# A two-layer recurrence with experts: column pairs, half-tile deal, fixed slots and paced loads

## The chip, the core and the metric

The kernel runs on one core of a Trainium2 chip. The time is the device time of one execution in microseconds (us). The median of the kernel before is 1176.22 us over three runs, from 1175.07 to 1176.29 us.

## What is computed

The input `x` has 16 sequences of 256 steps with 256 features. Four layers follow each other, each adding to `x`:

```
h_t = tanh(h @ Wh + x_t @ Wx + b)                       # plain recurrence, 256 steps
i,f,o,g = split(x_t @ Wx + b + h @ Wh)                  # LSTM, 256 steps
c = sigmoid(f)*c + sigmoid(i)*tanh(g);  h = sigmoid(o)*tanh(c)
out = gelu(x @ sw1 + sb1) @ sw2 + sb2                   # shared expert
    + sum over the 2 chosen of 4 experts: w * (gelu(x @ ew1[e] + eb1[e]) @ ew2[e] + eb2[e])
w = gelu(layernorm(cond) @ W1 + bias1) @ W2 + bias2     # low-rank parts of an adapter
x + up(gelu(down(x)))                                   # adapter, matrices per sequence
```

All products are made of float16 numbers: a float32 value is held as a high part (HI) and a remainder (LO), and one product takes three matmuls, HI by HI, LO weights by HI data, and HI weights by LO data.

## The kernel before, in words

**Two recurrences side by side.** Time is cut into 16 blocks of 16 steps (`U`). After a head that transposes `x` and runs the plain recurrence (RNN) on block 0, the main loop `block_steps` runs the LSTM on block `it`, the RNN on block `it + 1`, and the shared expert on block `it - 1`. Each of the 256 loop steps has the same skeleton.

- TensorE (`lstm_step`, `rnn_step`): 48 narrow matmuls of 16 columns for the eight LSTM gate tiles, then 12 for the RNN. It then adds wide work that depends on nothing recent: `fig_x` and `o_x` (the input parts of the LSTM gates, 64 and 128 columns), and tiles of the shared expert (`shared_hidden`, `shared_down`, six matmuls of 256 columns each) as the table `FILL` deals them. At the end of a block `rnn_x(it + 2)` makes the input part of a whole RNN block: 14 matmuls of 256 columns.
- ScalarE (L537, L541, L548): tanh of six gate tiles (`tfig`), tanh of the output gate (`to`), then `rnn_step` (L531, L532: `rf` in float32 and `RH` in float16), then tanh of the cell (`tc`), then whatever else the step has: seeds of PSUM banks (L555), two GELUs of a hidden tile (L581 into `gel`, L584 into `GH`), a weight piece to its high part (L497).
- VectorE (`lstm_step`, L846 to L858): `fc`, `ig` and the cell from `tfig`; after `tc` the high part of the hidden state (L851, semaphore `v_hh`), for which TensorE's next step waits, then its low part and the sum into `X`. Behind these stand remainders of hidden tiles (L824), remainders of weight pieces (L731), the splitting of `X` for the expert (L795, L798, at step 0), `add_y` (L818, at step 15).
- GpSimd: the low part of the RNN's hidden state (L406) and four small sums a step.

**Experts' weights.** Four experts have two matrices of 1 MB each. In blocks 1 to 8 one matrix per block is turned into HI and LO in eight pieces, at the steps 2, 4, 5, 6, 7, 9, 11 and 12 (`EXPERT_WINDOWS`). SyncE loads a whole matrix of 1 MB into `stage0` when the previous one is used up. In the same blocks, which I call matrix blocks, a part of the adapter's `W2` (1 MB, into `stage1`) is multiplied at steps 12 and 13 (`low_rank`, eight float32 matmuls), `add_bias` (VectorE, L946) and `low_hi` (ScalarE, L629) follow at step 14, and `low_lo` (VectorE, L952) at step 15. Blocks 9 to 13 have neither; I call them plain blocks.

**After the loop.** The gate chooses two experts per sequence, and these experts and the adapter follow, from about 754 us to the end. The change does not touch their code.

What orders the work is the program order on each engine and the semaphores between engines; there is no scheduler. Each engine takes its instructions in order.

Of the kernel before, what the change touches and what calls it, by code (L numbers as in the profile page):

```python
# [19 lines left out]
F32 = mybir.dt.float32  # L20
# [6 lines left out]
P = 128  # L27
B, T, D = 16, 256, 256
C = D // P
U = 16  # L30
NB = T // U
G = 8
# [25 lines left out]
def build_program(nc, a, out, scratch):  # L58
    ctx = ExitStack()
    with ctx:  # L60
# [35 lines left out]
        rf = sb("rf", [P, 2, C, B], F32)  # L96
        x1s = sb("x1s", [P, 2, C, B], F32)
# [58 lines left out]
        def late(*shape):  # L156
# [43 lines left out]
        names = """ld_stage0 ld_stage1 ld_small ld_first ld_cond ld_bias ld_rnn  # L200
# [4 lines left out]
            a_xr p_xr pe_rx pe_r a_rh  p_rlo p_x1 p_x1h p_x1l  # L205
# [38 lines left out]
        EXPERT_WINDOWS = (2, 4, 5, 6, 7, 9, 11, 12)  # L244
# [46 lines left out]
        def _(sp):  # L291
            with nc.allow_non_contiguous_dma(reason="small tables, once"):
# [35 lines left out]
                for j in range(2 * E):  # L328
                    def load_expert():

                        sp.wait_ge(s["v_wlo"], SHARED_SPLIT + j * N_MATRIX if j else LSTM_SPLIT + N_MATRIX)
                        src = a[("L2_cond_ew1", "L2_cond_ew2")[j % 2]][j // 2]
                        sp.dma_start(stage[0][:, :].rearrange("p (c n) -> p c n", c=(C, M)[j % 2]), wide(src)
                                     ).then_inc(s["ld_stage0"], 16)

                    if j == 0:
                        load_expert()
                        sp.wait_ge(s["v_wlo"], SHARED_SPLIT)
                    else:
                        sp.wait_ge(s["pe_w2"], j)  # L340
                        sp.wait_ge(s["v_low"], j)
                    for t in range(4):
                        at = j * 1024 + t * LOW_N
                        sp.dma_start(low_bias[32 * t:32 * t + 32, :],
                                     a["L3_cond_bias2"][at:at + LOW_N].partition_broadcast(2 * B)
                                     ).then_inc(s["ld_bias2"], 16)
                    sp.dma_start(w2_in, wide(a["L3_cond_W2"])[:, :, j * 1024:(j + 1) * 1024]
                                 ).then_inc(s["ld_stage1"], 16)
                    if j > 0:
                        load_expert()  # L350
# [133 lines left out]
        def _(act):  # L484
# [40 lines left out]
            def rnn_step(blk, r):  # L525
                n = blk * U + r
                z = RB[:, :].rearrange("p (m t b) -> p m t b", m=C, t=U)[:, :, r, :]
                act.wait_ge(s["pe_r"], n + 1)
# [30 lines left out]
            def seeds(it, u, last):  # L559

                if u % H == H - 1 and not (last and u >= U - 2 * H):
                    seed(it * U + u + 1, FIG[u // H % 2], slice(0, 6), H, "a_fig_seed")
                if u % G == G - 1 and not last:
                    seed(it * U + u + 1, OB[u // G], slice(6, 8), G, "a_o_seed")

            def x_hi(blk, c):

                act.wait_ge(s["pe_rx"], blk)
# [9 lines left out]
            def shared_gelu(tile, m):  # L578
                act.wait_ge(s["pe_h"], tile + 1)
                act.wait_ge(s["v_gl"], tile - 1)  # L580
                nc.scalar.activation(gel[:, m % 2, :], HB[m % 2][:, 0:256], ACT.Gelu_apprx_tanh,  # L581
                                     scale=1 / S_W1, bias=sb1[:, m:m + 1])
                act.wait_ge(s["pe_d"], tile - 3)
# [15 lines left out]
            def block_steps(it, first, last, matrix=False):  # L599
                for u in range(U):  # L600
                    lstm_gates(it, u)
                    if not last:
                        rnn_step(it + 1, u)
                    lstm_cell(it, u)
                    seeds(it, u, last)
                    if not first:
                        for kind, m in FILL[u]:
                            if kind == "h":
                                shared_gelu(it * M + m, m)
# [10 lines left out]
                    if matrix and u in EXPERT_WINDOWS:  # L620
                        i = EXPERT_WINDOWS.index(u)
                        if i == 0:
                            act.wait_ge(s["ld_stage0"], it * 16 + 32)
# [1001 lines left out]
```

## Time and profile before

| | us |
|---|---|
| median of three runs | 1176.22 |
| profiled execution | 1176.01 |
| its span, first to last instruction | 1174.2 |
| TensorE (PE) matmuls busy | 1131.0, 96% of the span |
| VectorE (DVE) busy | 764.5, 65% |
| ScalarE (ACT) busy | 605.2, 52% |
| GpSimd (POOL) busy | 366.3, 31% |
| mean granted TensorE clock | 0.967 of full |

A busy TensorE is not TensorE at its peak, since consecutive matmuls overlap in the records. The time of a stretch is therefore read from the distance between starts of instructions, not from the busy time. One `tfig` instruction of ScalarE stands for one step of the loop, so that the first and last start of a count of them gives the time of so many steps.

### The profile page before, as it was taken

What the parts mean: (1) busy time and instruction counts of PE and PEld (TensorE: products, weight loads), DVE (VectorE), ACT (ScalarE), POOL (GpSimd) and SP (SyncE); (2) the same over time, 40 slices, a digit from 0 to 9 for tenths busy, and PEclk for the clock granted to TensorE, in tenths of its full rate; (3) what the DMA queues carried; (4) which work ended last, traced back from release to release, by engine and by line L of the source; (5) the groups of instructions that cost most, each with busy time, mean ns of one, the idle gap of its engine ahead of it and who ended that gap; (6) DMA issues with size and microseconds to landing.
All of it is one profiled execution on the core that took longest, in us unless ns stands there. A gap on an engine that the chain in (4) does not pass through costs nothing. (4 is left out here: it accounts for less than half of the span.)

```text
span 1174.2 us, 58158 instructions
## 1 busy us (share of the span) xinstructions
PE 1131.0 (96%) x23706; PEld 1010.7 (86%) x23706; DVE 764.5 (65%) x2954; ACT 605.2 (52%) x2147; POOL 366.3 (31%) x1372
## 2 busy tenths in 40 slices
PE   5899999999999999999999999899999999999998
PEld 4788889889889888999999998778888888888877
DVE  6565666666666656556565557687666666667697
ACT  4455566566566555565555554533333333334476
POOL 3654344344434334444444441065000000000041
PEclk7759999999989989999999999899999999999999
DMA  8211202202202011110000000000000000000022
GB/s 245 75 44 40 80 4 81 79 5 80 68 16 80 25 59 26 14 15 14 4 4 5 4 5 4 3 2 1 2 2 2 2 2 2 2 3 2 3 76 87
DMA packets 44432, 37.14 MB, mean 32 GB/s; under 512 B 24280, under 2 KB 39946, under 8 KB 44172
## 3 DMA queue, kind: packets, MB, share of 16 engines
q1 hardware_dynamic: 43564, 33.12, 9.3%
q8 instruction: 194, 3.18, 1.1%
q14 instruction: 66, 0.54, 0.2%
q10 hardware_dynamic: 608, 0.30, 0.1%
HBM read 28.42 MB, written 4.98 MB: 28 GB/s over the span
## 5 line engine op out<-in xcount | busy, mean ns | idle before, releaser
L1285 PE MATMUL bank<-LH,seq 128*128 128x16 f16 x8192 | 282.8, 170 | 12.2 <-DVE LH L851 10.0
L1285 PEld LDWEIGHTS bank<-LH,seq 128*128 128x128 f16 x8192 | 248.1, 96 | 53.9 <-DVE LH L851 46.5
L575 ACT ACTIVATE gel<-bank,seq 128x256 f32<-128x256 f32 x256 | 121.2, 473 | 215.1 <-PE bank L1190 212.2
L1188 PE MATMUL bank<-XHL,WE 128*128 128x256 f16 x768 | 211.1, 275 | 5.2 <-issue 3.0
L1188 PE MATMUL bank<-GH,WE 128*128 128x256 f16 x768 | 210.3, 274 | 1.6 <-DVE GH L824 1.2
L1190 PE MATMUL bank<-XHL,WE 128*128 128x256 f16 x768 | 211.2, 275 | 0.0
L1189 PE MATMUL bank<-XHL,WE 128*128 128x256 f16 x768 | 211.1, 275 | 0.0
L1189 PE MATMUL bank<-GH,WE 128*128 128x256 f16 x768 | 210.3, 274 | 0.0
L1190 PE MATMUL bank<-GH,WE 128*128 128x256 f16 x768 | 210.1, 274 | 0.0
L1291 PE MATMUL bank<-LH,seq 128*128 128x16 f16 x4096 | 177.2, 169 | 1.7 <-issue 1.7
L406 POOL TENSOR_TENSOR RH<-rf,RH 128x32 f16<-128x32 f32 x256 | 64.5, 252 | 354.1 <-ACT RH L532 354.1
L537 ACT ACTIVATE tfig<-bank 128x96 f32<-128x96 f32 x256 | 65.5, 256 | 208.9 <-PE bank L1291 206.6
L1189 PE MATMUL bank<-seq 128*128 128x64 f16 (+2 forms) x1024 | 156.0, 211 | 1.1 <-issue 1.1
L1190 PE MATMUL bank<-seq 128*128 128x64 f16 (+2 forms) x1024 | 157.0, 211 | 0.0
L1188 PE MATMUL bank<-seq 128*128 128x64 f16 (+2 forms) x1024 | 154.5, 210 | 0.0
L831 DVE CAST GH<-gel 128x256 f16<-128x256 f32 x256 | 78.3, 306 | 102.0 <-ACT gel L575 101.3
L1291 PEld LDWEIGHTS bank<-LH,seq 128*128 128x128 f16 x4096 | 139.4, 96 | 1.4 <-issue 1.4
L476 POOL TENSOR_TENSOR seq<-X,seq 128x512 f16<-128x512 f32 x16 | 21.5, 1344 | 332.1 <-ACT seq L650 332.1
L846 DVE SCALAR_TENSOR_TENSOR fc<-tfig,c 128x32 f32<-128x32 f32 x256 | 48.8, 191 | 114.2 <-ACT tfig L537 108.9
L833 DVE TENSOR_TENSOR GH<-gel,GH 128x256 f16<-128x256 f32 x256 | 113.0, 441 | 8.7
L851 DVE SCALAR_TENSOR_TENSOR LH<-to,tc 128x32 f16<-128x32 f32 x256 | 51.7, 202 | 77.4 <-ACT tc L548 77.4
L1190 PEld LDWEIGHTS bank<-seq 128*128 128x128 f16 x1024 | 97.6, 100 | 3.3 <-issue 1.2
(198 smaller groups left out, 2469.0 us busy)
## 6 DMA issues: line engine op xcount, KB each, us to landing
stage<-in_L_cond_ew SPq DMA_DIRECT2D x8, 1024.0 KB, 8.5
stage<-in_L_cond_W SPq DMA_DIRECT2D x8, 1024.0 KB, 5.3
XHL<-in_x SPq DMA_DIRECT2D x8, 512.0 KB, 9.2
out<-WE SPq DMA_DIRECT2D x16, 256.0 KB, 2.1
stage<-in_L_cond_sw SPq DMA_DIRECT2D x2, 1024.0 KB, 5.4
scratch<-rows SPq DMA_DIRECT2D x96, 8.0 KB, 2.3
stage<-in_L_cond_Wx SPq DMA_DIRECT2D x1, 1024.0 KB, 9.6
stage<-in_L_cond_Wh SPq DMA_DIRECT2D x1, 1024.0 KB, 11.8
```

Source lines behind the costliest of these rows:

```text
L406: nc.gpsimd.tensor_tensor(RH[:, slot, LO], rf[:, slot], RH[:, slot, HI], ALU.subtract).then_inc(s["p_rlo"], 1)
L537: nc.scalar.activation(tfig[:], FIG[u // H % 2][:, 0:6 * H * B].rearrange("p (m t b) -> p m t b", m=6, t=H)[:, :, u % H, :], ACT.Tanh, sca ...
L575: nc.scalar.activation(gel[:, m % 2, :], banks[m % len(banks)][:, 0:256], ACT.Gelu_apprx_tanh, scale=scale, bias=bias).then_inc(s["a_g"], 1)
L831: V.tensor_copy(GH[:, m % 4, HI], gel[:, m % 2]).then_inc(s["v_gh"], 1)
L833: V.tensor_tensor(GH[:, m % 4, LO], gel[:, m % 2], GH[:, m % 4, HI], ALU.subtract).then_inc(s["v_gl"], 1)
L846: V.scalar_tensor_tensor(fc[:], tf, 1.0, c2[:], ALU.add, ALU.mult)
L851: V.scalar_tensor_tensor(hh, to[:], 1.0, tc[:], ALU.add, ALU.mult).then_inc(s["v_hh"], 1)
L1188: MM(out_, w(HI), x(HI), start=start, stop=False, skip_group_check=True)
L1189: MM(out_, w(LO), x(HI), start=False, stop=False, skip_group_check=True)
L1190: return MM(out_, w(HI), x(LO), start=False, stop=stop, skip_group_check=True)
L1285: MM(z, LW[:, h, 1, c, tile * P:(tile + 1) * P], LH[:, old, HI, c], start=False, stop=False, skip_group_check=True)
L1291: last = MM(z, LW[:, HI, 1, c, tile * P:(tile + 1) * P], LH[:, old, LO, c], start=False, stop=(c == C - 1), skip_group_check=True)
```

## The change

There are six edits.

1. **Column pairs.** For the RNN blocks from 1 on (`PAIR_FROM`), the matmuls HI weights by HI data and HI weights by LO data become one matmul with 32 columns: the data `RH[:, old, :, c]` are both halves, and the two results go to two halves of the PSUM bank. A step has 8 RNN matmuls in place of 12. VectorE adds the two results (`rnn_sum`, a reduction from PSUM into the new SBUF tile `rz`), and ScalarE's `rf` and `RH` read `rz` and wait for `v_rz`.
2. **`rnn_x` in halves.** Since a bank now holds half a block, `rnn_x` runs twice a block, ahead of the RNN's matmuls of steps 0 and 8, with 14 matmuls of 128 columns each.
3. **Half-tile deal.** `FILL` comes from `HALVES`: a half tile is three matmuls of 256 columns, and each step has 0 to 3 of them, ahead of `fig_x`. `o_x` of the second half block moves from step 0 to steps 3 and 5.
4. **Fixed ScalarE slots.** Between `to` and `tc` stands now either the second GELU of the tile that was finished one step earlier (`shared_hi`) or a weight piece; `rf` and `RH` come after `tc`; then the first GELU (`shared_full`).
5. **Expert pieces over thirteen blocks.** Five pieces per block, at steps 1, 5, 7, 9 and 11, from block 1 to 13.
6. **Paced loads.** A piece of 128 KB is loaded into its part of `stage0` when the piece eight before it is used up; `W2` comes in four loads of 256 KB in a row, at the end of a block.

```diff
-        EXPERT_WINDOWS = (2, 4, 5, 6, 7, 9, 11, 12)
+        EXPERT_WINDOWS = (1, 5, 7, 9, 11)
...
+                def load_piece(i):
+                    j, k = divmod(i, N_MATRIX)
+                    sp.wait_ge(s["v_wlo"], SHARED_SPLIT + i + 1 - N_MATRIX if j else LSTM_SPLIT + k + 1)
...
+                    sp.dma_start(stage[0][:, at], src).then_inc(s[f"ld_e{k}"], 16)
...
+                ahead = N_MATRIX
+                for it in range(1, NB - 1):
+                    for k in range(5):
+                        if ahead < total:
+                            load_piece(ahead)
+                            ahead += 1
+                        if it < 2 * E and k == 5 - 1:
+                            for q in range(4):
+                                load_low_part(it, q)
...
+                    z = rz[:]
+                    act.wait_ge(s["v_rz"], n + 1 - PAIR_FROM * U)
...
                     lstm_gates(it, u)
+                    if not first and u > 0:
+                        for m in done_tiles(u - 1):
+                            shared_hi(it * M + m, m)
+                    if it > 0 and u in EXPERT_WINDOWS:
...
+                            weight_hi(expert_piece(i // N_MATRIX, i % N_MATRIX))
+                    lstm_cell(it, u)
                     if not last:
                         rnn_step(it + 1, u)
-                    lstm_cell(it, u)
+                    if not first:
+                        for m in done_tiles(u):
+                            shared_full(it * M + m, m)
...
+            def rnn_sum(n):
+                if n < PAIR_FROM * U:
+                    return
+                pair = RB[:, :].rearrange("p (a m t b) -> p m t b a", a=2, m=C, t=G)[:, :, n % G]
+                dve.wait_ge(s["pe_r"], n + 1)
+                V.reduce_sum(rz[:], pair, AX_X).then_inc(s["v_rz"], 1)
...
                 V.scalar_tensor_tensor(c2[:], fc[:], 0.5, ig[:], ALU.mult, ALU.add).then_inc(s["v_c2"], 1)
+                if rnn and u % G:
+                    rnn_sum(n + U)
                 dve.wait_ge(s["a_tc"], n + 1)
...
                 V.tensor_tensor(hl, h2[:], hh, ALU.subtract).then_inc(s["v_hl"], 1)
+                if rnn and u % G == 0:
+                    rnn_sum(n + U)
...
-                        last = MM(z[:, m, r], RW[:, HI, 1, c, m * P:(m + 1) * P], RH[:, old, LO, c],
+                        last = MM(z[:, :, m, r % G], RW[:, HI, 1, c, m * P:(m + 1) * P], RH[:, old, :, c],
                                   start=False, stop=(c == C - 1), skip_group_check=True)
...
-                if rx:
-                    pe.wait_ge(s["a_rh"], it * U + 2 * U)
-                    rnn_x(it + 2)
...
+HALVES = [0, 3, 2, 2, 2, 2, 2, 3, 0, 3, 2, 3, 2, 3, 2, 1]
+O_STEPS = (3, 5)
+O_SEEDS = (0, 10)
-X_HI, X_LO = (4, 6), (8, 10)
+X_HI, X_LO = (10, 13), (12, 14)
```

`LOW_WINDOWS`, `ADD_WINDOW`, `HI_WINDOW` and `LO_WINDOW` (steps 12, 13, 14, 14 and 15) stay as they were.

On TensorE, at the border between two blocks, the kernel before has the input part of a whole RNN block between step 15 and step 0 (`LH` is the LSTM's hidden state, `RH` the RNN's, `seq` holds their weights):

```order
L1243 MATMUL bank<-ones_pad,bias_pad 128x256 [waits v_xr,a_rh]
L1188 MATMUL bank<-seq 128x256
L1189 MATMUL bank<-seq 128x256
L1190 MATMUL bank<-seq 128x256
L1285 MATMUL bank<-LH,seq 128x16 [waits v_hh]
L1285 MATMUL bank<-LH,seq 128x16 x23
L1259 MATMUL bank<-RH,seq 128x16 [waits a_rh]
L1259 MATMUL bank<-RH,seq 128x16 x7
L1265 MATMUL bank<-RH,seq 128x16 [waits p_rlo]
L1265 MATMUL bank<-RH,seq 128x16 x3
```

The changed kernel has half of it inside step 0, behind the LSTM's matmuls:

```order
L1352 MATMUL bank<-LH,seq 128x16 [waits v_hh]
L1352 MATMUL bank<-LH,seq 128x16 x23
L1299 MATMUL bank<-ones_pad,bias_pad 128x128 [waits v_rz,v_xr]
L1239 MATMUL bank<-seq 128x128
L1240 MATMUL bank<-seq 128x128
L1241 MATMUL bank<-seq 128x128
L1316 MATMUL bank<-RH,seq 128x16 [waits a_rh]
L1316 MATMUL bank<-RH,seq 128x16 x3
L1332 MATMUL bank<-RH,seq 128x2x16 [waits p_rlo]
L1332 MATMUL bank<-RH,seq 128x2x16 x3
```

Step 15 ends now with `fig_x` and `o_x`, and the next step's LSTM matmuls follow at once. (Rows that repeat are left out of both.)

On ScalarE, a step of the kernel before that has a hidden tile reads:

```order
L537 ACTIVATE tfig<-bank 128x96 [waits pe_fig]
L541 ACTIVATE to<-bank 128x32 [waits pe_o]
L531 ACTIVATE rf<-bank 128x32 [waits p_x1h,pe_r]
L532 ACTIVATE RH<-bank 128x32
L548 ACTIVATE tc<-c 128x32 [waits v_c2]
L581 ACTIVATE gel<-bank,sb 128x256 [waits v_gl,pe_h]
L584 ACTIVATE GH<-bank,sb 128x256 [waits pe_d]
```

The same engine in step 2 of a block of the changed kernel:

```order
L565 ACTIVATE tfig<-bank 128x96 [waits pe_fig]
L569 ACTIVATE to<-bank 128x32 [waits pe_o]
L620 ACTIVATE GH<-bank,sb 128x256 [waits pe_d]
L576 ACTIVATE tc<-c 128x32 [waits v_c2]
L559 ACTIVATE rf<-rz 128x32 [waits p_x1h,v_rz]
L560 ACTIVATE RH<-rz 128x32
L615 ACTIVATE gel<-bank,sb 128x256 [waits v_gl,pe_h]
```

The GELU into `GH` (of the tile finished in step 1) has taken the place of `rf` and `RH` ahead of `tc`.

On VectorE, steps 15 and 0 of a matrix block in the kernel before (`low_lo` and `add_y`, then the LSTM's part of step 0, then the splitting of `X`):

```order
L952 SCALAR_TENSOR_TENSOR rows<-low_f,rows 128x32x8 [waits a_low]
L818 SCALAR_TENSOR_TENSOR X<-bank,X 128x32x16 [waits pe_d]
L846 SCALAR_TENSOR_TENSOR fc<-tfig,c 128x32 [waits v_c2,a_fig]
L851 SCALAR_TENSOR_TENSOR LH<-to,tc 128x32 [waits a_tc]
L856 TENSOR_TENSOR LH<-h,LH 128x32 [waits v_h2]
L858 SCALAR_TENSOR_TENSOR X<-h,X 128x32 [waits p_x1]
L795 CAST XHL<-X 128x32x16 [waits v_x2]
L798 TENSOR_TENSOR XHL<-X,XHL 128x32x16 [waits v_x2p]
```

And in the changed kernel:

```order
L1003 SCALAR_TENSOR_TENSOR rows<-low_f,rows 128x32x8 [waits a_low]
L856 SCALAR_TENSOR_TENSOR X<-bank,X 128x32x16 [waits pe_d]
L892 SCALAR_TENSOR_TENSOR fc<-tfig,c 128x32 [waits v_c2,a_fig]
L899 SCALAR_TENSOR_TENSOR LH<-to,tc 128x32 [waits a_tc]
L904 TENSOR_TENSOR LH<-h,LH 128x32 [waits v_h2]
L880 TENSOR_REDUCE rz<-bank 128x32 [waits pe_r]
L908 SCALAR_TENSOR_TENSOR X<-h,X 128x32 [waits p_x1]
L833 CAST XHL<-X 128x32x16 [waits v_x2]
L836 TENSOR_TENSOR XHL<-X,XHL 128x32x16 [waits v_x2p]
```

The order is the same but for the new sum, which stands ahead of the splitting in steps 0 and 8 and ahead of L899 in the other steps.

## Rows read from the trace of the kernel before

**Rows 1.** Starts of ScalarE's `tfig`, one a step: blocks 1 to 8, blocks 9 to 13.

```profile
L537 ACT ACTIVATE tfig<-bank x129: 244/250/443, 91.8 to 460.0; 128x96 f32<-128x96 f32 x129
...
L537 ACT ACTIVATE tfig<-bank x81: 247/250/251, 460.0 to 673.7; 128x96 f32<-128x96 f32 x81
```

**Rows 2.** The same in block 7, a matrix block without a stall, and in block 8.

```profile
L537 ACT ACTIVATE tfig<-bank x17: 245/250/443, 366.5 to 411.1; 128x96 f32<-128x96 f32 x17
...
L537 ACT ACTIVATE tfig<-bank x17: 245/250/443, 411.1 to 460.0; 128x96 f32<-128x96 f32 x17
```

**Rows 3.** Timeline of a step of block 10: start us, us, engine line op, tiles, count.

```profile
514.73 0.75 PE L1285 MATMUL bank<-LH,seq 128*128 128x16 f16 x24
...
516.10 0.19 DVE L846 SCALAR_TENSOR_TENSOR fc<-tfig,c 128x32 f32<-128x32 f32 x1 [0.95 <-ACT tfig L537]
...
516.12 0.20 ACT L541 ACTIVATE to<-bank 128x32 f32<-128x32 f32 x1
...
516.24 0.19 PE L1188 MATMUL bank<-seq 128*128 128x64 f16 x1
...
516.41 0.27 PE L1188 MATMUL bank<-XHL,WE 128*128 128x256 f16 x1
...
516.42 0.19 DVE L849 SCALAR_TENSOR_TENSOR c<-fc,ig 128x32 f32<-128x32 f32 x1
...
516.65 0.23 ACT L548 ACTIVATE tc<-c 128x32 f32<-128x32 f32 x1
...
516.91 0.19 DVE L851 SCALAR_TENSOR_TENSOR LH<-to,tc 128x32 f16<-128x32 f32 x1 [0.29 <-ACT tc L548]
...
517.16 0.76 PE L1285 MATMUL bank<-LH,seq 128*128 128x16 f16 x24
```

**Rows 4.** Timeline of step 13's `low_rank` matmuls in block 7, and the start of step 14.

```profile
402.36 0.64 PE L1331 MATMUL bank<-stage,hidT 128*32 128x256 f32 x8
...
402.94 0.76 PE L1285 MATMUL bank<-LH,seq 128*128 128x16 f16 x24
```

**Rows 5.** Timeline of the border between blocks 6 and 7, VectorE and ScalarE.

```profile
359.73 0.19 DVE L846 SCALAR_TENSOR_TENSOR fc<-tfig,c 128x32 f32<-128x32 f32 x1 [0.55 <-ACT tfig L537]
...
361.20 0.41 DVE L946 TENSOR_TENSOR low_f<-bank,low_bias 128x256 f32<-128x256 f32 x1
...
361.64 1.33 ACT L629 ACTIVATE rows<-low_f 128x256 f16<-128x256 f32 x1 [1.13 <-DVE low_f L946]
...
363.09 0.19 DVE L846 SCALAR_TENSOR_TENSOR fc<-tfig,c 128x32 f32<-128x32 f32 x1 [1.48 <-ACT tfig L537]
...
364.64 1.31 DVE L952 SCALAR_TENSOR_TENSOR rows<-low_f,rows 128x256 f16<-128x256 f32 x1
...
365.57 0.90 DVE L818 SCALAR_TENSOR_TENSOR X<-bank,X 128x512 f32<-128x512 f32 x1
```

**Rows 6.** Timeline of TensorE's wait in block 8.

```profile
416.79 0.37 PE L1188 MATMUL bank<-XHL,WE 128*128 128x256 f16 x1 [2.44 <-issue]
```

**Rows 7.** Stretches around it: us, PE busy (x), PEclk, DMA share, GB/s.

```profile
412.00:414.00 2.00, 2.00 (x73) 1.00 1.00 339
...
416.00:418.00 2.00, 1.21 (x6) 0.50 0.08 22
```

**Rows 8.** Groups by line: engine op, shapes, count | busy us, mean ns | idle before.

```profile
L584 ACT ACTIVATE GH<-bank,sb 128x256 f16<-128x256 f32 x128 | 59.8, 467 | 0.0
...
L802 DVE TENSOR_REDUCE blocksum<-X 128x16 f32<-128x256 f32 x32 | 13.0, 412 | 0.0
...
L798 DVE TENSOR_TENSOR XHL<-X,XHL 128x512 f16<-128x512 f32 x15 | 10.4, 692 | 0.5
...
L795 DVE CAST XHL<-X 128x512 f16<-128x512 f32 x15 | 6.3, 419 | 0.0
```

**Rows 9.** Timeline of the end of block 0, TensorE at the lower clock.

```profile
87.66 0.42 PE L1243 MATMUL bank<-ones_pad,bias_pad 128*128 128x256 f16 x1
...
90.64 0.81 PE L1285 MATMUL bank<-LH,seq 128*128 128x16 f16 x24
```

More of the change, by code:

```diff
@@ new lines, in _ @@
+                total = 2 * E * N_MATRIX
+                for i in range(N_MATRIX):
+                    load_piece(i)
+                for k in range(4):
+                    load_low_part(0, k)
+                ahead = N_MATRIX
[7 more added lines that the diff above has]
+                                load_low_part(it, q)
@@ L619, in block_steps @@
                         low_hi(it - 1)
[L620 to L623, printed above, removed]
-                        weight_hi(expert_piece(it - 1, i))
             def low_hi(g):
@@ L873, in _ @@
             for r in range(U):
+                rnn_sum(r)
                 for _ in range(LSTM_PIECES[r]):
@@ L956, in block_steps @@
                 for u in range(U):
-                    lstm_step(it, u)
+                    lstm_step(it, u, not last)
                     if last and u in extras:
@@ L1252, in rnn_step @@
                 old = (r + 1) % 2
-                z = RB[:, :].rearrange("p (m t b) -> p m t b", m=C, t=U)
-                if not isinstance(n, int) or n > 0:
+                z = RB[:, :].rearrange("p (a m t b) -> p a m t b", a=2, m=C, t=G)
+                if r % G == 0 and n > 0:
+                    rnn_x(blk, r // G)
+                if n > 0:
                     pe.wait_ge(s["a_rh"], n)
@@ L1416, in spread_logits, with block_steps @@
                    skip_group_check=True).then_inc(s["pe_gate"], 1)
-            def block_steps(it, first, last, rx, matrix=False):
+            def block_steps(it, first, last, matrix=False):
                 for u in range(U):
@@ L1426, in block_steps @@
                         logits()
+                    if not first:
+                        for kind, m, halves in FILL[u]:
+                            if kind == "h":
+                                shared_hidden(it - 1, m, halves)
+                            else:
+                                shared_down(it - 1, m, halves)
                     if u == 0:
@@ L1435, in block_steps @@
                             fig_x(it * (U // H) + u // H + 1, i)
-                    if u == 0:
-                        for i in range(C):
-                            o_x(2 * it + 1, i)
+                    if u in O_STEPS:
+                        o_x(2 * it + 1, O_STEPS.index(u))
                     if u == U - 1 and not last:
@@ L1580, in _, with fill_table, done_tiles @@
             adapter_steps(pe, step)
-FILL = [[] for _ in range(U)]
-for _m in range(M):
-    FILL[max(2 * _m - 1, 1)].append(("h", _m))
-    FILL[min(2 * _m + 2, 14)].append(("d", _m))
+HALVES = [0, 3, 2, 2, 2, 2, 2, 3, 0, 3, 2, 3, 2, 3, 2, 1]
+O_STEPS = (3, 5)
+def fill_table():
+    jobs = [("h", 0), ("h", 1)] + [job for m in range(2, M) for job in (("h", m), ("d", m - 2))]
+    jobs += [("d", M - 2), ("d", M - 1)]
+    stream = [(kind, m, c) for kind, m in jobs for c in range(C)]
+    table, at = [], 0
+    for n in HALVES:
+        step = {}
+        for kind, m, c in stream[at:at + n]:
+            step.setdefault((kind, m), []).append(c)
+        table.append([(kind, m, tuple(cs)) for (kind, m), cs in step.items()])
+        at += n
+    assert at == len(stream)
+    return table
+FILL = fill_table()
+def done_tiles(u):
+    return [m for kind, m, halves in FILL[u] if kind == "h" and C - 1 in halves]
 N_SCRATCH = 16 * Q * C * 3 * 4
```

173 lines of the change are left out of this document (98 added, 75 removed).

## The prediction

> **What bounds the kernel now.** I first read the starts of `tfig`, because one of them marks one loop step [rows 1]. 128 steps of blocks 1 to 8 take 460.0 - 91.8 = 368.2 us, 46.0 a block; 80 steps of blocks 9 to 13 take 213.7, 42.74 a block. Block 7, a matrix block, takes 44.6 [rows 2], so the eight matrix blocks together hold 368.2 - 8 x 44.6 = 11.4 us of something irregular.
>
> Next the timeline of one light step [rows 3]. TensorE starts it at 514.73. The 60 narrow matmuls last until 516.24, 1.51 us or 25 ns each; six of 64 columns last 0.17 (29 ns each); the six of 256 columns then need 6 x 0.109 = 0.65 (14 of them took 2.98 us at the lower clock [rows 9], 213 ns each; half of that is 107). TensorE is out of work at 517.07 and starts the next step at 517.16, when the high part of the hidden state is there: `fc` 1.37 after the step's first matmul, the cell 0.32 later, `tc` 0.23 later, the hidden state 0.26 later, TensorE 0.25 later. So a step lasts the larger of TensorE's work and a chain of 2.43 us, which I call the floor. Steps with little fill stand at the floor, steps 1, 14 and 15 lie far above it (work of 3.0, 3.2 and 3.9 us by these prices). With these prices, the largest of work and floor per step adds up to 42.2 for a plain block; 42.74 is measured, so 0.5 is not explained.
>
> Last the irregular part. In block 8 TensorE stands still for 2.44 us before 416.79 with the releaser "issue", so for nothing that another engine had to do [rows 6], just after a stretch in which the DMA engines are 100% busy, at 339 GB/s, with two loads of 1 MB; afterwards the granted clock is 0.50 [rows 7]. I read it as TensorE's own instructions arriving late behind the bulk loads.
>
> **The change, part by part.** The sum is made against the profiled execution, 1176.0 us, 0.2 below the median of the runs.
>
> *A plain block.* Pairs take four matmuls from each step: narrow work 56 x 0.025 = 1.40. The wide work is the same but dealt otherwise (128 columns taken at 55 ns, between the 29 and 109 of rows 3). Steps 0 and 8: 1.40 + 14 x 0.055 + 12 x 0.029 = 2.52. Even steps 2, 4, 6, 10, 12, 14: 1.40 + 0.35 + 0.65 = 2.40, so the floor of 2.43 holds. Odd steps 1 to 13: 1.40 + 0.17 + 0.98, or with two halves and one `o_x` tile 1.40 + 0.17 + 0.65 + 0.33, both 2.55. Step 15: 1.40 + 0.17 + 0.33 + 0.66 = 2.56. Sum 5.04 + 14.6 + 17.85 + 2.56 = 40.05. Two new waits come on top:
> - Step 1. In step 0 `rnn_sum` stands ahead of VectorE's splitting of `X`, whose 0.42 + 0.69 [rows 8] just fitted before the next `fc`. Splitting now ends about 2.8 after step 0's `fc`, while the next `fc` (2.52 after it) and the first hidden matmul want to start earlier; TensorE and the cell lose about 0.3.
> - Step 2. The tile h2 needs the bank of h0, and h0's second GELU now runs in step 2's slot: it can start only after `to`, 1.39 into the step, and lasts 0.47 [rows 3, 8], so it ends at 1.96 or later. TensorE wants the bank at 1.40 + 0.33 = 1.73. With the semaphore 0.3.
>
> I add 0.2 for what the model missed before: 40.9 a block, 1.85 less. Five blocks: -9.2. Block 14 I take at -0.4.
>
> *A matrix block.* It adds `low_rank`, 2 x 0.58 [rows 4], and a loss at the border that `rnn_x` and the double fill hid before. Step 14's `fc` starts at 359.73 [rows 5], `add_bias` 1.47 later, `low_hi` 0.44 after that, and it holds ScalarE so that `fc` of step 15 starts 3.36 after the former. TensorE had 3.2 of work there; now it has 2.40, and the floor would allow 2.43: loss 0.93. Then `low_lo` starts 1.55 after `fc`, `add_y` follows and ends at 365.57 + 0.90 = 366.47, 3.38 after it. TensorE had 3.9 of work and has now 2.56: loss 0.8. Together 1.75. So 40.9 + 1.2 + 1.75 = 43.85 a block. Eight blocks: 350.8. The irregular 11.4 is left out of this, since a load is never more than 1 MB at once, half of before. Block 1 starts at the lower clock, and its step 0 and part of step 1 now have wide work there: +2. Together 352.8, against 368.2: -15.4.
>
> *Block 0 and the head.* Both run mostly at the lower clock. `rnn_x(2)`, 90.64 - 87.66 = 2.98 [rows 9], leaves block 0; steps 0 and 8 take 14 matmuls of 107 ns each, 1.5, and come to 1.40 + 0.64 + 1.5 = 3.55 against 2.5: -1.0 in all. `rnn_x(1)`, as long, leaves the head, but GpSimd's last low part holds what follows for half of it: -1.5, and the first `rnn_x`, half as long, gives 0.5.
>
> Sum: -9.2 - 0.4 - 15.4 - 1.0 - 2.0 = -28.0, so **1148 us**.
>
> *What the trace doesn't show.* The price of a 32-column matmul into two pieces of a bank lies between that of 16 columns, 25 ns, and 64 columns, 29 ns [rows 3]; at 29 it is 4 x 0.004 x 16 = 0.26 a block, 3.6 in all. I take 25, since the spacing hardly grows with four times the columns. The Trainium skill, "TensorE: Matmul & The Clock Gate", section "Wait — 56ns, not 53.3ns?", states a start-to-start floor of about 25 ns, and 25 ns for 32 columns; by it the term is nought, and no run before shows that width.
>
> `rnn_sum` lasts from 0.19, like L851 [rows 3], to 0.41, like the reduction L802 that reads four times as much [rows 8]. It sits between the cell, from 516.42 for 0.19, and L851 at 516.91: 0.30 of idle time. I take 0.22, near the lower row because of its size: nothing. At 0.41 it puts 0.11 on the six steps at the floor and little on the others: +0.7 a block, 10 in all. Below nothing it can't be, since `tc` waited for the cell before as well. The GELU in the slot starts about 0.1 after `to` and blocks ScalarE to about 516.7, while `tc` started at 516.65: from 0 to 0.1 in the steps that have it; I take 0 and leave 4 us to the range. In the step, ScalarE's `rf` and `RH` come 0.4 later, with GpSimd behind them; TensorE needs them 1.2 into the next step, which still leaves 0.8.
>
> **The rivals.**
> - *R1, no loss at borders and slots.* If VectorE and ScalarE overlap more than I take, the 8 x 1.75 and part of the 14 x 0.6 are not paid: 1148 - 14 - 5 = 1129. For it: L818 starts 0.93 after L952, which is listed with 1.31. Against it: `fc` in rows 5 really starts 3.36 after the former.
> - *R2, the clock falls at the borders.* TensorE waits there for 1.75 of 6.7 us. The one long wait of rows 6 was followed by clock 0.50 [rows 7], and block 8 with 48.9 is 4.3 over block 7 [rows 2] with a wait of 2.5: 1.7 for the clock. Eight times: 1148 + 14 = 1162. Against it: the waits are short and spread over two steps. The Trainium skill, same page, section "HAM oscillation — how this bites in real kernels", has it that gaps between groups of matmuls bring the clock down; the trace agrees only for the one long gap.
> - *R3, instructions still come late.* `W2` is still 1 MB in a row. If half of the 11.4 stays, with its clock: 1154.
> - *R4, slower.* The recurrence, not TensorE, becomes the bound everywhere. Place: `rnn_sum` between the cell and L899, which waits for `pe_r` and so for TensorE. If it ends 0.32 too late (0.62 long, or as late), the floor is 2.75: a plain block 44.3, a matrix block 44.3 + 0.6 + 1.75 = 46.7, in all +15, 1191. It decides from a floor of 2.67 on, 0.24 above today's, a sum of 0.54. Against it: `pe_r` comes about 1.6 into the step, 0.2 after `fc` starts, and a reduction of four times the size lasts 0.41.
> - *R5, it doesn't do what it says*: pairs save nothing because every step stands at a raised floor just under 2.67: 1176.
>
> **How the numbers follow.** Forecast 0.55, R1 0.13, R2 0.10, R3 0.13, R4 0.06, R5 0.03. Faster by over 0.2% (about what a measurement of this kernel can tell from no change; 2.4 us): 0.91; within: 0.03; slower: 0.06. The range leaves out R4, R5 and the far half of R1: 1133 to 1165; its upper end holds R2 with a little of the reduction's 10.
>
> **What would show it.** The count of TensorE matmuls falls by 736 (15 blocks lose 64, 16 gain 14); `tfig` starts 40.9 apart per plain block and 43.9 per matrix block; no "issue" wait over 0.3 in blocks 1 to 8; low-clock stretches only up to block 1 and at the loop's end; step 15's `fc` in matrix blocks 3.4 after step 14's, and step 0's 3.4 after that. I am wrong if plain blocks are over 42 (a raised floor) or if matrix blocks are nearer to plain ones than 2 us (R1).

## The result, and the profile after

The changed kernel takes 1147.85 us (median, 1146.71 to 1149.13), the kernel before 1176.26 (1175.07 to 1177.61) beside it. The ratio is 0.9758, with a 95% interval of 0.9742 to 0.9775: 28.4 us less, where 28 were forecast. The profiled execution took 1146.71 us, its span 1144.9. From the page of the profile after, engine, busy us, share and count, and the granted clock in 40 slices:

```profile
PE 1098.0 (96%) x22970; PEld 1004.3 (88%) x22970; DVE 803.9 (70%) x3194; ACT 601.1 (53%) x2147; POOL 395.3 (35%) x1372
...
PEclk8759999999999999999999999899999999999999
```

The matmul count has fallen from 23706 to 22970, by 736 as worked out ahead. The starts of `tfig` in blocks 1 to 8, in block 7 and in blocks 9 to 13 (count, duration in ns, first and last start in us), which answer to [rows 1, 2]:

```profile
L565 ACT ACTIVATE tfig<-bank x129: 251/251/571, 87.9 to 436.5; 128x96 f32<-128x96 f32 x129
...
L565 ACT ACTIVATE tfig<-bank x17: 251/251/565, 349.2 to 392.8; 128x96 f32<-128x96 f32 x17
...
L565 ACT ACTIVATE tfig<-bank x81: 251/251/252, 436.5 to 642.0; 128x96 f32<-128x96 f32 x81
```

From the same starts, with all blocks in the order of the program:

| part | before | after | difference | predicted |
|---|---|---|---|---|
| head, to the first `tfig` | 47.8 | 44.7 | -3.1 | -2.0 |
| block 0 | 44.0 | 43.2 | -0.8 | -1.0 |
| blocks 1 to 8 | 368.2 | 348.6 | -19.6 | -15.4 |
| blocks 9 to 13 | 213.7 | 205.4 | -8.2 | -9.2 |
| block 14 | 41.3 | 40.7 | -0.6 | -0.4 |
| block 15 | 38.6 | 40.7 | +2.1 | 0 |
| from its last `tfig` on | 420.6 | 421.6 | +0.9 | 0 |
| span | 1174.2 | 1144.9 | -29.3 | -28.0 |

A step at the floor, here the fifth of block 10 in the timeline after; it answers to [rows 3]:

```profile
488.58 0.75 PE L1352 MATMUL bank<-LH,seq 128*128 128x16 f16 x24
...
489.96 0.19 DVE L892 SCALAR_TENSOR_TENSOR fc<-tfig,c 128x32 f32<-128x32 f32 x1 [0.38 <-ACT tfig L565]
...
490.28 0.19 DVE L895 SCALAR_TENSOR_TENSOR c<-fc,ig 128x32 f32<-128x32 f32 x1
...
490.39 0.22 DVE L880 TENSOR_REDUCE rz<-bank 128x32 f32<-128x64 f32 x1
...
490.51 0.23 ACT L576 ACTIVATE tc<-c 128x32 f32<-128x32 f32 x1
...
490.77 0.19 DVE L899 SCALAR_TENSOR_TENSOR LH<-to,tc 128x32 f16<-128x32 f32 x1 [0.16 <-ACT tc L576]
...
491.02 0.43 PE L1352 MATMUL bank<-LH,seq 128*128 128x16 f16 x11
```

The chain is 1.38 + 0.32 + 0.23 + 0.26 + 0.25 = 2.44, as before. `rnn_sum` (L880) lasts 0.22 and fits into the idle time of VectorE: 0.16 of that time is left before L899. The border of blocks 8 and 9 in the timeline after, VectorE, ScalarE and TensorE, answers to [rows 5]; a bracket holds the idle time before the instruction and what ended it:

```profile
430.92 0.19 DVE L892 SCALAR_TENSOR_TENSOR fc<-tfig,c 128x32 f32<-128x32 f32 x1 [0.93 <-ACT tfig L565]
...
432.93 1.34 ACT L667 ACTIVATE rows<-low_f 128x256 f16<-128x256 f32 x1 [0.98 <-DVE low_f L997]
...
434.38 0.19 DVE L892 SCALAR_TENSOR_TENSOR fc<-tfig,c 128x32 f32<-128x32 f32 x1 [0.97 <-ACT tfig L565]
...
435.44 0.76 PE L1352 MATMUL bank<-LH,seq 128*128 128x16 f16 x24 [0.72 <-DVE LH L899]
435.84 1.36 DVE L1003 SCALAR_TENSOR_TENSOR rows<-low_f,rows 128x256 f16<-128x256 f32 x1
...
436.82 0.89 DVE L856 SCALAR_TENSOR_TENSOR X<-bank,X 128x512 f32<-128x512 f32 x1
...
437.63 0.18 DVE L892 SCALAR_TENSOR_TENSOR fc<-tfig,c 128x32 f32<-128x32 f32 x1
...
438.68 0.76 PE L1352 MATMUL bank<-LH,seq 128*128 128x16 f16 x24 [0.53 <-DVE LH L899]
...
439.57 0.77 DVE L836 TENSOR_TENSOR XHL<-X,XHL 128x512 f16<-128x512 f32 x1
...
440.26 0.25 DVE L892 SCALAR_TENSOR_TENSOR fc<-tfig,c 128x32 f32<-128x32 f32 x1
```

`fc` of step 15 comes 3.46 after that of step 14, `fc` of step 0 3.25 after that, and TensorE waits 0.72 and 0.53 for the hidden state. Before, it did not wait at that place; the input part of the RNN block filled the time. In step 1, `fc` stands directly behind the splitting of `X` (L836), 2.63 after step 0's.

TensorE's waits in blocks 1 to 8, first of the kernel before, then after (line <- what ended the wait: us in total, times, longest):

```profile
PE bank L1285 <- DVE LH L851: 3.1, 8, 0.4
PE bank L1188 <- issue: 2.4, 1, 2.4
PE bank L1291 <- issue: 1.7, 2, 1.4
PE bank L1265 <- issue: 1.4, 1, 1.4
PE bank L1189 <- issue: 1.1, 1, 1.1
PE bank L1285 <- issue: 0.8, 1, 0.8
```

```profile
PE bank L1352 <- DVE LH L899: 9.4, 16, 0.7
PE bank L1239 <- DVE XHL L836: 0.2, 1, 0.2
```

7.4 us of "issue" are gone, and 16 waits of about 0.6, two for each border, have come. (The waits of 0.4 in the first list stand at step 8 of a block, not at a border.) The weights' loads after (count, KB each, us to landing):

```profile
stage<-in_L_cond_ew SPq DMA_DIRECT2D x64, 128.0 KB, 2.4
stage<-in_L_cond_W SPq DMA_DIRECT2D x32, 256.0 KB, 3.6
```

Last, the stretch behind the border shown (us, busy us of the engines, granted clock, DMA share, GB/s):

```profile
436.00:440.60 4.60, 3.92 (x125) 3.69 (x122) 4.20 (x14) 2.06 (x9) 2.31 (x7) 1.00 0.02 4
440.60:444.00 3.40, 3.40 (x71) 2.91 (x69) 1.39 (x9) 1.31 (x6) 1.86 (x8) 0.50 0.15 42
```

Behind one of eight borders the clock is at its lower level (1.2 GHz) for 3.4 us; step 1 of block 9 lasts 3.82 there (from TensorE's first matmul of a step to that of the next), where the other blocks behind a border have 2.88. Blocks 10 to 13 take 40.71 each, block 9 took 42.56; about 0.8 of that belongs to the border itself (with the second GELU moved, below, block 9 has no lower clock and takes 41.3 against 40.5).

### The profile page after: what moved, and what is told of

The parts are those of the page before. It is cut to its first block and busy times, and to the rows that moved or that the text cites. A ratio compares the mean times of both kernels' runs of the same rounds, so it can differ in the third digit from the quotient of the medians.

```text
span 1144.9 us, 57020 instructions
## 1 busy us (share of the span) xinstructions
PE 1098.0 (96%) x22970; PEld 1004.3 (88%) x22970; DVE 803.9 (70%) x3194; ACT 601.1 (53%) x2147; POOL 395.3 (35%) x1372
## 3 DMA queue, kind: packets, MB, share of 16 engines
q1 hardware_dynamic: 54060, 33.12, 10.2%
## 5 line engine op out<-in xcount | busy, mean ns | idle before, releaser
L1352 PEld LDWEIGHTS bank<-LH,seq 128*128 128x128 f16 x8192 | 244.2, 96 | 30.2 <-DVE LH L899 23.5
L1241 PE MATMUL bank<-seq 128*128 128x64 f16 (+2 forms) x1088 | 164.5, 208 | 0.0
L1240 PE MATMUL bank<-seq 128*128 128x64 f16 (+2 forms) x1088 | 163.1, 208 | 0.0
L1239 PE MATMUL bank<-seq 128*128 128x64 f16 (+2 forms) x1088 | 161.5, 208 | 0.0
L1358 PEld LDWEIGHTS bank<-LH,seq 128*128 128x128 f16 x4096 | 139.2, 96 | 0.0
L1239 PEld LDWEIGHTS bank<-seq 128*128 128x128 f16 x1088 | 105.2, 100 | 3.4 <-issue 0.2
L1240 PEld LDWEIGHTS bank<-seq 128*128 128x128 f16 x1088 | 103.4, 100 | 3.2
```

The costliest lines, as they stand in the source:

```text
L1239: MM(out_, w(HI), x(HI), start=start, stop=False, skip_group_check=True)
L1240: MM(out_, w(LO), x(HI), start=False, stop=False, skip_group_check=True)
L1241: return MM(out_, w(HI), x(LO), start=False, stop=stop, skip_group_check=True)
L1352: MM(z, LW[:, h, 1, c, tile * P:(tile + 1) * P], LH[:, old, HI, c], start=False, stop=False, skip_group_check=True)
L1358: last = MM(z, LW[:, HI, 1, c, tile * P:(tile + 1) * P], LH[:, old, LO, c], start=False, stop=(c == C - 1), skip_group_check=True)
```

## The experiments

All medians are compared with the kernel before on the same chip (1175.1 to 1177.9 us). "Plain" and "matrix" block are those of the prediction; the times of blocks and steps are distances between starts in the one profiled execution of each kernel. No run takes back the spreading of the expert pieces over thirteen blocks, or the order of `tc`, `rf` and `RH`, by itself.

### Without pairs

```diff
-PAIR_FROM = 1
+PAIR_FROM = NB
```

> The changed kernel with PAIR_FROM at the number of blocks: every RNN step has its 12 narrow matmuls again and no sum on VectorE; ScalarE reads the bank. All else stays. Theory (TensorE's work per step against a floor of 2.43 us): the steps above the floor gain four matmuls of 25 ns, 0.10 us, the even ones 0.08; 1.5 us in a plain block (40.7 to 42.2), 1.2 in a matrix block, whose border steps wait for other engines: 18 us in all, 1166. Rival (the pairs bring little, since the sum on VectorE and the later rf and RH cost about what they save; the gain came from the deal and the slots): under 1153.

Measured: 1163.86 us (1162.42 to 1164.57), ratio 0.9907 (0.9878 to 0.9936). So the pairs are worth 16 us; 18 were expected. `tfig` in blocks 1 to 8 and 9 to 13:

```profile
L565 ACT ACTIVATE tfig<-bank x129: 251/251/574, 88.4 to 446.9; 128x96 f32<-128x96 f32 x129
...
L565 ACT ACTIVATE tfig<-bank x81: 251/251/252, 446.9 to 657.0; 128x96 f32<-128x96 f32 x81
```

A plain block at full clock takes 41.8 instead of 40.7 (the sum of its steps), where I had 42.2; the five together take 210.1 instead of 205.4. Most steps are 0.08 to 0.1 longer, four matmuls of 25 ns. Five of the six light steps are 2.51 instead of 2.43, where they were stopped by the floor; the sixth, step 2, is 2.69 in both, so its wait does not come from the pairs. Step 1 is 2.66 like the other odd steps, while with pairs it is 2.78 where the others are 2.57: the wait in step 1 comes with the pairs. That `rnn_sum` makes it is an inference from its place ahead of the splitting, since the four matmuls more in each step cover 0.1 of such a wait too.

### Whole tiles instead of half tiles

```diff
-HALVES = [0, 3, 2, 2, 2, 2, 2, 3, 0, 3, 2, 3, 2, 3, 2, 1]
+HALVES = [0, 2, 2, 2, 2, 2, 2, 2, 2, 2, 2, 2, 2, 2, 4, 2]
```

> The changed kernel with whole tiles only in the deal (steps 1 to 13 one tile each, step 14 two, step 15 one, steps 0 none). Theory: the odd steps fall to the floor, while step 8 has 3.17 us of work and step 14 3.06; a plain block goes from 40.7 to about 41.3. In a matrix block steps 14 and 15 have 3.06 and 2.88 of work beside low_hi and low_lo, which cost 1.75 before and now 0.8: 43.3 in place of 43.7. Together +1, so 1149, no measurable change. Rival (the even deal is what brings most of the gain): 1155 or more.

Measured: 1156.92 us (1154.18 to 1160.33), ratio 0.9838 (0.9806 to 0.987). The rival's number came, my 1149 did not. Plain blocks were as I had it (41.6, mine 41.3), and the one matrix block that ran wholly at full clock behind a border took 43.8 (mine 43.3). But behind seven of the borders stood a stretch of 3.4 us at the lower clock, like this one (columns as above):

```profile
182.00:185.40 3.40, 3.40 (x72) 2.97 (x70) 2.21 (x13) 2.21 (x10) 1.91 (x8) 0.50 0.15 45
```

Each cost 0.7 to 0.8 us: such a matrix block takes 44.5 to 44.6. The expectation had no term for it. TensorE waited only once at each of these borders, 0.5 to 0.7 us at step 0.

### The kernel before with its two loads apart

```diff
+                    load_expert()
                     if j == 0:
-                        load_expert()
                         sp.wait_ge(s["v_wlo"], SHARED_SPLIT)
...
-                    if j > 0:
-                        load_expert()
```

> The kernel before, with SyncE's load of the next expert matrix issued ahead of its wait for the adapter's product, so that it goes out at step 12 and W2's load at step 14, about 6 us apart instead of back to back; nothing else is changed. Theory: no wait with the releaser issue is left in blocks 2 to 8 and the irregular 11.4 us goes: 1165. Rival (1 MB at once is already enough to hold the instructions up): 1172 to 1176.

Measured: 1167.09 us (1165.84 to 1168.66), ratio 0.9936 (0.9918 to 0.9954). TensorE's waits and `tfig` in blocks 1 to 8:

```profile
PE bank L1283 <- DVE LH L849: 3.3, 9, 0.4
PE bank L1263 <- issue: 0.9, 1, 0.9
PE bank L1186 <- issue: 0.6, 1, 0.6
```

```profile
L535 ACT ACTIVATE tfig<-bank x129: 243/250/446, 90.5 to 449.3; 128x96 f32<-128x96 f32 x129
```

The blocks take 358.8 instead of 368.2, and neither of the two stretches of 6.8 us at the lower clock that the kernel before has in them (one of them in [rows 7]) is left. So 9.4 of the irregular 11.4 us of the profiled executions came from the two loads of 1 MB standing together; on the medians of all runs it is 8.0. I had expected no wait for "issue" at all, and two are left.

The trace of the kernel before shows how the loads hold TensorE up. The DMA queue q8 carries instructions, in packets of 16 KB. Between 404 and 416 us, around the wait of [rows 6], it has (packets, MB, share of 16 engines):

```profile
q8 instruction: 2, 0.03, 1.1%
```

In the 12 us from 380 us on there are three. In blocks 1 to 8 its packets start 4.4 us apart (median). Only six distances are over 6 us; they are 7.3 to 9.2 long, and each of them lies across a burst of the two loads. These six go with the six waits for "issue": each wait ends 2.2 to 2.5 us after the start of the packet that was so long in coming. At the border of blocks 6 and 7 a packet started in the middle of the burst, and TensorE did not wait. With the loads apart, the two waits that are left stand behind the two distances over 7 us (7.4 and 7.1). That q8 serves TensorE fits its counts over the whole kernel: 194 packets before, 188 after, 196 without pairs, rising and falling with the matmuls. So the instructions did come late, and what counts is how long a burst keeps the next packet from starting.

### One more megabyte in the burst

```diff
+                            sp.dma_start(spare[it], a["L3_cond_W2"][0:P, 0:2048]).then_inc(s["ld_spare"], 16)
```

It stands behind W2's loads of blocks 1 to 7, from HBM to HBM.

> The changed kernel, and behind the four loads of W2 at the end of blocks 1 to 7 one more load of 1 MB, from HBM to an unused place in HBM; no engine waits for it before block 13. Theory (TensorE's instructions come late behind 2 MB of loads in a row): waits with the releaser issue come back in blocks 2 to 8, each with 0.5 to 2.6 us, some with a stretch at the lower clock: +5 to +11, 1153 to 1159. Rival (the stalls before came from the waits of the large loads themselves, on stage0): no change, 1148.

Measured: 1153.7 us (1149.83 to 1156.8), ratio 0.9817 (0.9778 to 0.9856), an interval that lies only just above that of the kernel after. The size is that of the theory, the form is not. TensorE's waits in blocks 1 to 8, and one of five stretches behind borders:

```profile
PE bank L1355 <- DVE LH L902: 9.5, 16, 0.7
PE bank L1355 <- issue: 0.8, 1, 0.8
PE bank L1242 <- issue: 0.5, 2, 0.3
```

```profile
226.00:229.40 3.40, 3.40 (x60) 2.81 (x61) 1.58 (x9) 1.15 (x6) 2.09 (x9) 0.50 0.87 328
```

There is little "issue", but there are five borders with the lower clock, about 0.8 to 1.3 us each. Blocks 1 to 8 take 5.2 us more than in the kernel after: 0.9 of it is block 2, which has the wait of 0.8 and no lower clock, and 4.3 are the four blocks with the lower clock, one of which also has the wait of 0.3. The packets of q8 were held up as long as in the kernel before: at three borders two starts are 8.7 to 9.5 us apart. Either the waits at the border hid most of that, or these loads cost mainly by the clock. Two runs further down look at this.

### The row copies inside the next block

`low_hi` and `low_lo`, 1.34 and 1.36 us at the border, are halved and moved to steps 4, 6 and 5, 7 of the next block.

```diff
-                    if matrix and u == HI_WINDOW:
-                        low_hi(it - 1)
+                    if 2 <= it <= 2 * E + 1 and u in LOW_HI_STEPS:
+                        low_hi(it - 2, LOW_HI_STEPS.index(u))
...
-ADD_WINDOW, HI_WINDOW, LO_WINDOW = 14, 14, 15
+ADD_WINDOW = 14
+LOW_HI_STEPS, LOW_LO_STEPS = (4, 6), (5, 7)
```

> The changed kernel with low_hi (ScalarE, 1.33 us) and low_lo (VectorE, 1.31 us) cut in halves and moved from steps 14 and 15 of their block to steps 4 and 6 (ScalarE, at the step's end) and 5 and 7 (VectorE, at the step's end) of the next block, where ScalarE has neither a GELU nor a seed. Theory (the border of a matrix block loses 1.75 to 1.8 us to them, and sometimes a stretch at the lower clock): a matrix block falls from 43.7 to plain block plus low_rank, 41.9, and step 15's first matmul waits no longer: -14, 1134. Rival (they only use time that something else, low_rank's and the fill's placing, would cost as well): -4 or less, 1144 or more.

Measured: 1134.37 us (1133.17 to 1135.11), ratio 0.9645 (0.9618 to 0.9672). `tfig` in blocks 1 to 8 and 9 to 13:

```profile
L565 ACT ACTIVATE tfig<-bank x129: 250/250/252, 87.7 to 424.8; 128x96 f32<-128x96 f32 x129
...
L565 ACT ACTIVATE tfig<-bank x81: 250/250/252, 424.8 to 628.5; 128x96 f32<-128x96 f32 x81
```

The longest `tfig` fell from 571 to 252 ns, for it no longer runs beside a border copy. A matrix block from 2 on takes 42.1 instead of 43.65, and there is no wait of TensorE and no lower clock in them. The border is worth 1.57 us; I had 1.75. (In block 15, which has none of these copies, there is a lower clock as in the kernel after.)

### `fig_x` ahead of the half tiles in steps 1 and 2

```diff
+FIG_FIRST = (1, 2)
...
+                    if u not in FIG_FIRST:
+                        fill()
```

> The changed kernel with fig_x ahead of the half tiles in steps 1 and 2 of each block, so that h0 and h2 start 0.17 and 0.35 us later in their steps. Theory (step 1 waits for the splitting of X, which stands behind rnn_sum, and step 2 for the bank of h0, freed by the GELU in the slot): step 1 goes from 2.78 to 2.6, step 2 from 2.69 to 2.44 in plain blocks, the same in matrix blocks: 14 x 0.4 = -6, 1142. Rival (both steps are bound by VectorE's own queue, the splitting ahead of fc, not by TensorE's wait): step 1 stays at 2.78, and -3.5 or less in all.

Measured: 1140.17 us (1138.43 to 1142.0), ratio 0.9689 (0.9658 to 0.9719). In plain blocks step 1 goes from 2.78 to 2.61 or 2.72, step 2 from 2.69 to 2.44. So both new waits were real. A plain block is 0.3 shorter for it, 40.3 to 40.5, which makes 4.6 in 14 blocks; the rest comes mainly from the lower-clock stretches of blocks 9 and 15, which this execution does not have in their steps. There was no lower clock between blocks 2 and 15, though the two waits at each border were as long as after (10.2 us in 16): where the clock falls is not decided by them alone.

### The second GELU directly behind the first

```diff
-                    if not first and u > 0:
-                        for m in done_tiles(u - 1):
-                            shared_hi(it * M + m, m)
...
                             shared_full(it * M + m, m)
+                            shared_hi(it * M + m, m)
```

> The changed kernel with the second GELU of a tile directly behind the first one again, at the end of the step, in place of the next step's slot; weight pieces and the order of tc, rf and RH stay. Theory: ScalarE has about 1.2 us between RH and the next tfig; two GELUs occupy 0.37 each and a seed 0.42, so steps with both (3, 7, 11) just fit; h0's bank is free earlier and step 2 loses its wait of 0.25. Together -3.5, 1144. Rival (the fixed slot carries the gain, because GELUs at the end push tfig back): +5 or more, 1153.

Measured: 1147.05 us (1143.03 to 1149.44), ratio 0.9745 (0.9709 to 0.9782), no change that can be told from the kernel after. Steps 1 and 2 of a plain block together fell from 5.47 to 5.22, as expected: a plain block takes 40.47. But three borders had the lower clock, one of them here:

```profile
267.00:270.40 3.40, 3.40 (x73) 2.91 (x71) 1.65 (x9) 1.77 (x7) 1.88 (x8) 0.51 0.14 40
```

They took about 1.0 each and gave the gain back. In the four executions of this kernel the mean clock runs from 0.958 (1149.4 us) to 0.971 (1143.0 us), so the number of such stretches seems to differ from execution to execution, and one profile of a kernel does not tell how many it has on average. That the second GELU stands in the slot between `to` and `tc` is no gain of the change; the slot of the weight pieces was not tried.

### Row copies moved and `fig_x` ahead

The two edits together.

> The edits of the two kernels with low_hi and low_lo moved and with fig_x first in steps 1 and 2 together. Theory: they touch different steps and add up, -14 - 6, 1128. Rival (moving one uncovers the other): less than the larger of the two alone plus 2.

Measured: 1129.28 us (1127.74 to 1129.4), ratio 0.9595 (0.9568 to 0.9622). It is the fastest version, 18.6 us under the kernel after; the parts, 13.5 and 7.7, nearly add up. Blocks 2 to 8 take 41.65 to 41.82. From block 1's steps to block 15's the clock is full:

```profile
92.00:685.00 593.00, 590.65 (x17134) 561.21 (x17131) 441.61 (x2154) 371.94 (x1560) 293.24 (x1119) 1.00 0.12 33
```

### The extra megabyte, and the loads in one burst, without the waits at the border

Both start from the version with the row copies moved. The first has the extra load of above. The second has W2's loads ahead of the five expert pieces, so that all nine are issued one behind the other within some 6 us.

```diff
+                    if it < 2 * E:
+                        for q in range(4):
+                            load_low_part(it, q)
                     for k in range(5):
                         if ahead < total:
                             load_piece(ahead)
                             ahead += 1
-                        if it < 2 * E and k == 5 - 1:
-                            for q in range(4):
-                                load_low_part(it, q)
```

> The kernel of e4_low_moved (low_hi and low_lo in halves inside the next block, 1134.4 us, TensorE hardly waits at the borders) with the extra load of e3_double_burst: 1 MB more behind W2's loads in blocks 1 to 7. In e3 the extra load cost 5.9 us, but only one 'issue' wait showed; my reading was that TensorE waits for the row copies at the border anyway and late instructions hide behind that wait. Theory A (the border wait hid them): now each of seven borders shows 'issue' waits of TensorE of 0.5 to 2.5 us, as in the kernel before (9 us in all), and the time is 1134 + 6 to 10 = 1140 to 1144. Rival B (bulk loads do no harm once the experts' loads stand apart, the cost of e3 was the granted clock alone, which fell because TensorE waited at the border): no 'issue' waits over 0.3, no stretch of low clock between blocks 2 and 15, under 1137.

> The kernel of e4_low_moved with the pacing undone as far as the buffers allow: SyncE issues the four loads of W2 first and the block's five expert pieces directly behind them, so some 1.6 MB start together at a block's border and nothing loads within the block. Theory A (instructions for TensorE arrive late behind loads of over 1 MB in a row): 'issue' waits at several borders, 1 to 5 us in all, 1136 to 1139. Rival B: under 1136, no 'issue' wait over 0.3 us.

Measured: 1136.15 us (1133.94 to 1136.36), ratio 0.9653 (0.9634 to 0.9671), and 1135.37 (1132.45 to 1136.48), ratio 0.9639 (0.9614 to 0.9663), against 0.9645 without either. TensorE's waits for "issue" in blocks 1 to 14, first with the extra load, then with the burst:

```profile
PE bank L1363 <- issue: 1.6, 2, 1.0
PE bank L1244 <- issue: 0.2, 1, 0.2
```

```profile
PE bank L1242 <- issue: 0.5, 1, 0.5
```

The numbers are those of the rival: waits for "issue" of 1.8 and 0.5 us in all, where the theory had a cost of 6 to 10 for the first and waits of 1 to 5 for the second; only the rival's "no wait over 0.3" did not hold. The waits in blocks 6 and 7 of the first run cost 1.2 and 0.7 us. Neither run has the lower clock between blocks 2 and 14. But the runs do not refute the theory that late instructions are the cause, for the instructions were far less late in them. The three waits over 0.3 stand behind packets of q8 that start 5.5 to 7.2 us apart, and the longest distance at a border is 6.2 in the first and 7.2 us in the second, against 9.5 with the extra load on the kernel after and 9.2 in the kernel before. By these rows a burst of this size does harm or not by the moment at which it meets the next packet. In the profiled executions, without waits at the border, neither the extra load nor the burst brought the lower clock. So the larger part of the extra load's cost on the kernel after came by way of the clock, about 4 of the 5.2 us in blocks 1 to 8; about 1 us was a late packet.

## Why the prediction was right

**The sum.** 28.0 forecast, 28.4 measured on the medians. The errors of the terms cancel to 1.3 us of the profiled execution, and that they cancel is luck: the head and blocks 1 to 8 gave 5.3 more than forecast, while block 15 and the rest took back 3.0, and blocks 9 to 13 gave 1.0 less. So each is looked at.

*The pairs.* The step model held: 40.71 for an undisturbed plain block (40.9 forecast), floor 2.43 to 2.44, `rnn_sum` 0.22. The 32-column matmuls follow each other at 25 ns (in the step of block 10 shown above four of them start at 489.89 and what follows starts at 489.99); the Trainium skill's figure for that width, named in the prediction, agrees. Neither 29 ns for them nor 0.41 for the reduction came. Their worth is shown by the run without pairs: 16 us.

*The new waits in steps 1 and 2.* I took 0.3 each. The steps last 2.78 and 2.69 where their neighbours of the same work last 2.57 and 2.43: 0.21 and 0.26. The run without pairs shows that the first comes with the pairs and the second does not, the run with `fig_x` ahead that TensorE had been waiting in both, and the one with the second GELU behind the first that step 2's hangs on the slot.

*The border.* 1.75 forecast, 1.57 shown by the run with the row copies moved, worth 13.5 us in all. The distances of `fc` were to be 3.4 and 3.4; they are 3.46 and 3.25 at the border shown, and 3.34 and 3.25 at most others.

*The irregular part.* "The irregular 11.4 is left out" was right: no wait for "issue" over 0.3 is left in blocks 1 to 8. The run of the kernel before with its loads apart shows that distance between the loads alone removes 9.4 of it. The reading that TensorE's instructions arrive late behind the bulk loads is borne out by the packets of q8: the six waits of the kernel before stand behind the six packets that came over 6 us after their predecessor. In the changed kernel, where a burst keeps the DMA engines full for 2.5 to 3 us instead of 5 to 6, two distances are still over 7 us (7.2 and 7.7), but both lie at borders where TensorE waits for the hidden state anyway. No run made the late packets happen again at their old size without the waits at the border.

*Where the size was off.* "Block 1 starts at the lower clock: +2" did not come: the clock was up again after 89.0 us, and block 1 takes 43.03, less than its neighbours. With matrix blocks at 43.65 instead of 43.85, this makes the -15.4 a -19.6. The head's -3.1 against -2.0 is hardly a miss: over the ten profiles of kernels with the new head it lies between 44.6 and 47.0, 45.7 on average, and the two profiles with the old head have 47.8 and 46.9, so that it gives 1.6 on average.

*Block 15, at 0 forecast, costs 2.1.* I had not looked at it step by step. VectorE in its steps 4 and 5, before and then after:

```profile
726.39 0.18 DVE L846 SCALAR_TENSOR_TENSOR fc<-tfig,c 128x32 f32<-128x32 f32 x1
...
727.76 1.39 DVE L893 TENSOR_REDUCE part<-XHL 128x32 f32<-128x160 f16 x4
729.07 0.18 DVE L846 SCALAR_TENSOR_TENSOR fc<-tfig,c 128x32 f32<-128x32 f32 x1
```

```profile
694.19 0.18 DVE L892 SCALAR_TENSOR_TENSOR fc<-tfig,c 128x32 f32<-128x32 f32 x1
...
695.56 1.39 DVE L944 TENSOR_REDUCE part<-XHL 128x32 f32<-128x160 f16 x4
696.87 0.41 DVE L862 TENSOR_TENSOR GH<-gel,GH 128x256 f16<-128x256 f32 x1
697.20 0.18 DVE L892 SCALAR_TENSOR_TENSOR fc<-tfig,c 128x32 f32<-128x32 f32 x1
```

`fc` stands behind the reduction in both. In the new deal a hidden tile is finished in that step, and its subtraction L862 stands there too: 3.01 instead of 2.68 from `fc` to `fc`. Steps 7 and 11 lose 0.3 each; I did not follow them up. Step 9 lasts 3.46 in a stretch at the lower clock, about 1 of the 2.1: without pairs, with `fig_x` ahead and with the second GELU moved it lasts 2.45 at full clock. No run tried to win back the 0.3 us in steps 5, 7 and 11.

**The rivals.** R1 (no loss at the borders) is refuted: the loss was there, and moving it away gave 1134. R2 (the clock falls at the borders) did not decide, but was no fancy: it fell behind one border after, behind seven with whole tiles, five with the extra load, three with the GELU moved, one without pairs, none with `fig_x` ahead, and with the row copies moved behind none in four kernels. One time costs 0.7 to 1.3 us, where I had 1.7: these stretches last 3.4 us, the one that I had priced lasts 6.8. My reason against it, that the waits are short, was too weak: waits of 0.5 to 0.7 are enough in some executions. Nor was the long wait of [rows 6] the only one in the kernel before that went with a lower clock: a wait of 1.15 us in block 6 did too. R3 and R4 did not come, nor did R5.

## What to carry to other kernels

Model a step as the larger of TensorE's work and the recurrence's chain, from prices between starts of instructions; then look for the instructions that are tied to a place and lose their cover when TensorE's work there goes. Here that cost 1.57 us at each of eight borders, and spreading two copies over light steps gave back 13.5 us in all. When an order of work is dealt anew, the first and last block, with duties of their own, want the same look as the steady ones. And a short wait that recurs can have a second price beside its length, the lower clock behind it, so that an edit that saves 0.25 in a block can lose it again elsewhere. Last, when TensorE waits for nothing that another engine does, look at the DMA queue of its instructions beside the bulk loads.

## What the runs showed of the hardware

- Weight load and matmul follow each other every 25 ns at 32 columns, every 55 to 56 ns at 128 and every 109 to 111 ns at 256 (in the kernel after, blocks 10 and 11).
- The granted clock was at 0.50 in stretches behind borders where TensorE had waited once or twice for 0.5 to 0.7 us, not each time and not at the same borders in two kernels: 1 of 8 borders after, 7 with whole tiles, none with `fig_x` ahead. With the waits gone, it stayed full from block 2 to block 14 in the profiles of all four kernels.
- Two loads of 1 MB next to each other cost the kernel before 9.4 us in eight blocks (8.0 on the medians), by waits of TensorE that no other engine ended and by the clock behind them. One megabyte more, in one load, cost 0.0059 of the ratio in the kernel with waits at its borders, and 0.0008, inside the intervals, in the one without.
- Instructions come in packets of 16 KB on a DMA queue of their own, one every 4.4 us in blocks 1 to 8 of the kernel before. A burst of 2 MB put two starts 7.3 to 9.2 us apart at six borders, and TensorE stood still for 0.3 to 2.4 us at each of them, until 2.2 to 2.5 us after the late packet's start.
- A copy of 256 columns into transposed places of `rows` takes 1.34 us on ScalarE; half of it, 128 columns, takes 0.76 on average.
